# A graph attention layer on one core: index work and node projections become one stage, each partition holds 13 consecutive tiles, and the borders between tiles cross partitions by matrix products

## The reference

```
q, k, v = layer_norm(x @ Wq), layer_norm(x @ Wk), layer_norm(x @ Wv)      # nodes, by head
ke, ve  = layer_norm(edge_attr @ Wke), layer_norm(edge_attr @ Wve)        # edges, by head
rel_k = layer_norm(concat(ke, k[src]) @ relk_W + relk_b)
qk    = sum(q[dst] * rel_k) / 4
lse   = logsumexp of qk over the edges of one dst
rel_v = layer_norm(concat(ve, v[src]) @ relv_W + relv_b)
agg   = segment_sum((qk - lse[dst]) * rel_v, dst)
z     = layer_norm(relu(agg @ z_W + z_b))
out   = layernorm(x + z)
```

## Time and profile before

| | |
|---|---|
| median of 3 runs | 3415.34 us |
| the profiled execution's own time | 3418.76 us |
| its span | 3417.0 us |
| PE busy | 2971.2 us (87% of the span) |
| DVE busy | 3060.6 us (90%) |
| ACT busy | 2326.8 us (68%) |
| POOL busy | 2483.4 us (73%) |
| PE's granted clock, mean | 0.928 of 2.4 GHz |

### The profile page before, as it was taken

How to read it: one execution, slowest core, us unless ns; L and a number is a source line. 1 busy time by engine, 2 the same in 40 slices (tenths; PEclk the granted TensorE clock), 3 DMA queues, 4 the chain that set the end, 5 groups by cost and what they waited for, 6 DMA issues and landing times. The chain is left out here.

```text
span 3417.0 us, 75946 instructions
## 1 busy us (share of the span) xinstructions
PE 2971.2 (87%) x18966; PEld 2581.6 (76%) x19162; DVE 3060.6 (90%) x4202; ACT 2326.8 (68%) x5281; POOL 2483.4 (73%) x1886
## 2 busy tenths in 40 slices
PE   0335599999999999999999999999999999967698
PEld 0313488888888888888888888888888888854465
DVE  5545499999999999999999999999999999987555
ACT  0015478787887888787878788888878887853333
POOL 1527688888888888888888888888888888842660
PEclk6569799999999999999999999999999999998855
DMA  6143588888888888888888888888888888855431
GB/s 81 32 48 119 150 250 248 251 246 250 247 250 247 251 245 251 248 249 249 247 249 248 249 247 251 245 250 247 250 247 250 246 250 248 248 185 159 115 86 42
DMA packets 692637, 723.74 MB, mean 212 GB/s; under 512 B 125638, under 2 KB 586875, under 8 KB 691929
## 3 DMA queue, kind: packets, MB, share of 16 engines
q1 hardware_dynamic: 596163, 503.11, 47.5%
q0 software_dynamic: 84896, 211.67, 23.5%
q10 hardware_dynamic: 11511, 8.18, 1.3%
HBM read 483.77 MB, written 238.10 MB: 211 GB/s over the span
## 5 line engine op out<-in xcount | busy, mean ns | idle before, releaser
L1194 POOL DMA_INDIRECT e_rows<-node_table,e_gcol x1564 | 2178.7, 1393 | 482.2 <-issue 477.4
L1017 PE MATMUL banks<-w_edge,e_eat 128*128 128x240 f32 x6256 | 1399.3, 367 | 3.3 <-DVE e_p L1262 3.0
L1017 PEld LDWEIGHTS banks<-w_edge,e_eat 128*128 128x128 f32 x6256 | 1181.5, 190 | 113.5 <-DVE e_p L1262 11.8
L1010 PE MATMUL banks<-e_h,e_oh 128*128 128x256 f32 x3128 | 826.4, 387 | 8.2 <-ACT e_agg L1095 4.2
L1245 DVE TENSOR_REDUCE e_zs<-e_z 128x96 f32<-128x1440 f32 x391 | 646.2, 1653 | 0.6 <-issue 0.3
L1010 PEld LDWEIGHTS banks<-e_h,e_oh 128*128 128x128 f32 x3128 | 534.1, 191 | 51.9 <-DVE e_h L1270 5.1
L1095 ACT ACTIVATE e_agg<-banks 128x512 f32<-128x512 f32 x782 | 464.9, 594 | 104.3 <-PE banks L1010 104.0
L1280 DVE TENSOR_REDUCE e_yvar<-e_ysq 128x64 f32<-128x960 f32 x391 | 448.1, 1146 | 40.4 <-ACT e_ysq L1125 40.4
L1262 DVE TENSOR_TENSOR e_p<-banks,e_yr 128x960 f32<-128x960 f32 x391 | 448.9, 1148 | 3.2 <-PE banks L1017 3.2
L1270 DVE TENSOR_TENSOR e_h<-e_p,e_zw 128x960 f32<-128x960 f32 x391 | 449.2, 1149 | 0.1
L1210 DVE TENSOR_TENSOR e_p<-e_p,e_rows 128x960 f32<-128x960 f32 x391 | 449.1, 1149 | 0.0
(11 more groups left out here) (369 smaller groups left out, 2794.6 us busy)
## 6 DMA issues: line engine op xcount, KB each, us to landing
tile_sums<-e_agg SPq DMA_DIRECT2D x391, 512.0 KB
e_q<-q_by_rank SPq DMA_DIRECT2D x1564, 96.0 KB
e_ea<-in_edge_attr SPq DMA_DIRECT2D x390, 256.0 KB
e_rows<-node_table,e_gcol POOLq DMA_INDIRECT x1564
edge_lse<-t_lse_sb SPq DMA_DIRECT2D x14, 448.0 KB, 3.4
edge_qk<-e_qkt SPq DMA_DIRECT2D x130, 48.0 KB
node_table<-n_tb SPq DMA_DIRECT2D x24, 240.0 KB
t_x<-edge_qk SPq DMA_DIRECT2D x2, 2240.0 KB
```

The source lines that it names most:

```text
L1010: last = nc.tensor.matmul(agg_ps[:, (j % 2) * AW:(j % 2 + 1) * AW], oh[:, x % OR, j, :], hh[:, x % HR, j, :, :, :].rearrange("p h s d -> p ...
L1017: last = nc.tensor.matmul(out_ps[:, j // 2, (j % 2) * 2 * HC:(j % 2 + 1) * 2 * HC], eat[:, x % 4, j * P:(j + 1) * P], t["w_edge"][:, at:at ...
L1194: g.indirect_dma_start(out=rows[:, k, j, :], out_offset=None, in_=table, in_offset=bass.IndirectOffsetOnAxis(ap=gcol[:, kb, at:at + 1].bit ...
```

## The change

`prologue` and `nodes` become one phase, `start`, with one barrier fewer.

- Layout: partition p holds the 13 consecutive tiles 13p to 13p + 12. Loads are one contiguous run in each partition. A tile's neighbour is mostly the next column of the same partition; at a partition's border the value comes by a PE product with a shifted identity (`identx`). The running sums over tiles are made in each partition (13 long), then over the 128 partition totals in one row, and go back by a product with a one. `tile_ends`, `tile_bases` and `first_edge` in DRAM are gone; the next node's first edge (`lbn_ps`) is a product too.
- The search for a node's tile has 14 columns in place of 129, in three pieces (`PICKS`) in place of 17.
- The gathers of `hits` have a buffer for all 49 blocks in place of three rings of four, and DVE's counting is spread over the turns of the node loop (`SET_AT`). `rank_row` is made in turn 18 (`LB_AT`), and all scatters of q come after it. q's three parts for all nodes are held in `room_b`.
- The node loop is unrolled. The table's bias is added by DVE instead of POOL; the third part of q is written by DVE instead of ACT. Casts of the rank features, the flags, the carry keys and their stores lie in the loop's turns. The weights' evictions and the casts of `dst` and `src` are ACT's.
- `edges`: `e_feat` and `rank_code` have 5 partitions instead of 128; DVE sets them and the other constants, and the load of `e_gcol` goes ahead of the wait for that.

```diff
-            for i in range(3):
-                sp.dma_start(t["tile_d"][i:i + 1, 0:2], below[i:i + 1, :]).then_inc(s_tep, 16)
...
-            for i, (which, at) in enumerate(((0, 2), (0, 1), (0, 3), (1, 2), (1, 1), (1, 0), (2, 2), (2, 1))):
-                sp.dma_start(tl[:, i, :], t["tile_d"][which, at:at + ROWS].rearrange("(k e) -> k e", e=P)).then_inc(s_tl, 16)
...
-            sp.dma_start(t["lb_d"].rearrange("(b p) -> p b", p=P), lb[:]).then_inc(s_lbst, 16)
-            sp.wait_ge(s_lbst, 16)
-            sp.dma_start(lb_next[:, 0:BLOCKS - 1], t["lb_d"][1:1 + whole].rearrange("(b p) -> p b", p=P)).then_inc(s_lbn, 16)
...
+            parts = lambda ap, lo, hi: ap[lo * ROWS:hi * ROWS].rearrange("(p e) -> p e", e=ROWS)
+            sp.dma_start(flat(dst_i[0:LOW]), parts(a["dst"], 0, LOW)).then_inc(s_dst, 16)
...
+            nc.tensor.matmul(shift_ps[:, 0:KT], identx[:, 0:P], lastx[:, 2:KT + 2], start=True, stop=True)
...
+            nc.tensor.matmul(car_ps[:, 0:1], car_row[0:1, 0, 0:P], t["one_c"][0:1, 0:1], start=True, stop=True)
...
+    PICKS = [(0, 12), (12, 36), (36, BLOCKS)]
+    SET_AT = {5 * k // 4 + 2: k for k in range(SETS)}
+    LB_AT = 5 * (SETS - 1) // 4 + 3
...
+                if c == LB_AT:
+                    pe.wait_ge(s_lb, 1)
+                    nc.tensor.matmul(lbn_ps, identx[:, 2:P + 2], lb[:, 0:BLOCKS], start=True, stop=False)
+                    nc.tensor.matmul(lbn_ps, corner[:], lb[0:1, 1:BLOCKS + 1], start=False, stop=True).then_inc(s_lbn, 1)
...
+            pool.wait_ge(s_idx, 1)
+            for n in range(NP):
+                b, nb, rows = pair(n)
+                pool.wait_ge(s_1, n + 1)
+                pool.wait_ge(s_2, n + 1)
+                pool.wait_ge(s_3, n + 1)
+                for b2 in range(b, b + nb):
+                    g.indirect_dma_start(out=t["q_rank"], ..., in_=qp[0:rows, b2, :], ...).then_inc(s_sc, 16)
...
-        nfeat = sb_mid("rank_code", [P, P], bf16)
+        nfeat = sb_mid("rank_code", [5, P], bf16)
...
-    feat = sb("e_feat", [P, FB, BE], bf16)
+    feat = sb("e_feat", [5, FB, BE], bf16)
...
+                        sp.dma_start(gcol[:, kb, :], t["cols"][:, bass.ds(BATCH * TILES * b, BATCH * TILES)]).then_inc(s_ft[kb], 16)
+                        if not loop and c == 0:
                             sp.wait_ge(s_init, INIT)
                         sp.dma_start(feat[0:3, kb, :], t["feat_d"][:, bass.ds(BE * b, BE)]).then_inc(s_ft[kb], 16)
-                        sp.dma_start(gcol[:, kb, :], t["cols"][:, bass.ds(BATCH * TILES * b, BATCH * TILES)]).then_inc(s_ft[kb], 16)
...
-            g.memset(feat[:], 0.0).then_inc(s_init, 1)
-            pool.wait_ge(s_init, 1)
-            g.memset(feat[0:5, :, :], 1.0).then_inc(s_init, 1)
-            g.memset(p[:, :, :, :, :, C:D], 1.0).then_inc(s_init, 1)
-            g.memset(hh[:, :, :, :, 0, C:D], 1.0).then_inc(s_init, 1)
...
+            v.memset(feat[:], 1.0).then_inc(s_init, 1)
+            v.memset(p[:, :, :, :, :, C:D], 1.0).then_inc(s_init, 1)
+            v.memset(hh[:, :, :, :, 0, C:D], 1.0).then_inc(s_init, 1)
```

More of the change, by code:

```diff
@@ new lines, in start @@
+    s_u, s_tb, s_qs, s_q = sem("nodes_scaled"), sem("nodes_table"), sem("nodes_q_scaled"), sem("nodes_q")
+    s_1, s_r1, s_2, s_3 = sem("nodes_part1"), sem("nodes_rest1"), sem("nodes_part2"), sem("nodes_part3")
+    CONSTS, MASKS = 25 + C, 9
+    SMALLS = 5 + 2 + 2 + 10 + 3
+    first = [banks[:, 3 * k:3 * k + 2, :] for k in range(2)]
+    second = [banks[:, 3 * k + 2, :] for k in range(2)]
+    x_ps = banks[:, 6, :]
+    shift_ps, car_ps, e16_ps = bank[2][:, 0:KT + 3], bank[2][:, 3 * P:3 * P + 2], bank[2][:, 3 * P + 8:3 * P + 10]
@@ new lines, in start, with picked, pair @@
+    locT_ps = bank[2][0:1, P:3 * P]
+    rel_ps, col_ps = bank[0][:, 0:4 * C + 4 + D], bank[0][:, P:P + 10]
+    src_ps = [bank[5], bank[6], bank[7], bank[1][:, P:2 * P]]
+    lbn_ps, pre_ps = bank[7][:, 0:BLOCKS], bank[7][:, P:P + 2 * BLOCKS]
+    def picked(b0, b1):
+        w = KT + 1
+        return bank[3 + PICKS.index((b0, b1)) % 2][:, 0:(b1 - b0) * w].rearrange("p (b c) -> p b c", c=w)
+    def pair(n):
+        if not 0 <= n < NP:
+            return None
+        return (2 * n, 2, P) if n < PAIRS else (BLOCKS - 1, 1, LAST)
@@ L294, in _ @@
+            for k in range(3):
+                sp.wait_ge(s_tst[k], 16 * len(range(k, NP, 3)))
+            sp.wait_ge(s_ri, 16)
+            sp.wait_ge(s_ki, 16)
             sp.wait_ge(s_nf, 16 * 5)
-            sp.wait_ge(s_rt, 16 * 2)
+            sp.wait_ge(s_st, 16 * 9)
         @block.gpsimd
@@ L481, in _, with count @@
[L481 to L486 removed]
+            def count(k):
                 nb = min(SLOTS, BLOCKS - SLOTS * k)
                 bs = slice(SLOTS * k, SLOTS * k + nb)
[L489 removed]
+                dve.wait_ge(s_hit[k], 16 * nb)
@@ L714, in body @@
+                last = nc.tensor.matmul(bank[7][:, (2 + i) * HC:(3 + i) * HC], w_ct[:, 3 + i, :], bdg[:, 2 * i, :], start=True, stop=True)
+            last.then_inc(s_prod, 1)
+            pe.wait_ge(s_t, len(PICKS))
+            pe.wait_ge(s_wev, 10)
+            for c in range(NP + 1):
+                n = c - 1
+                if pair(n):
+                    b, nb, rows = pair(n)
                     pe.wait_ge(s_xc, n + 1)
-                    if loop or x >= 2:
+                    if n >= 2:
@@ L718, in body @@
                     for c2 in range(nb):
-                        nc.tensor.matmul(first[k][0:rows, c2, 0:3 * HC + F], xt[:, k, c2, 0:rows], t["w_node"][:, 0:3 * HC + F], start=True, stop=True)
-                        last = nc.tensor.matmul(second[k][0:rows, c2 * 2 * HC:(c2 + 1) * 2 * HC], xt[:, k, c2, 0:rows], t["w_node"][:, 3 * HC + F:NW],
+                        nc.tensor.matmul(first[n % 2][0:rows, c2, 0:3 * HC + F], xt[:, n % 2, c2, 0:rows], t["w_node"][:, 0:3 * HC + F], start=True, stop=True)
@@ L721, in body @@
+                        last = nc.tensor.matmul(second[n % 2][0:rows, c2 * 2 * HC:(c2 + 1) * 2 * HC], xt[:, n % 2, c2, 0:rows], t["w_node"][:, 3 * HC + F:NW],
                                                 start=True, stop=True)
                     last.then_inc(s_pr, 1)
-                if pair(c, i, loop):
-                    n, k, b, nb, rows = pair(c, i, loop)
-                    pe.wait_ge(s_x[k], 16 * use(c, i))
-                    if loop or c >= 1:
+                n = c
+                if pair(n):
+                    b, nb, rows = pair(n)
+                    pe.wait_ge(s_x[n % XR], 16 * (n // XR + 1))
+                    if n >= 1:
```

1040 lines of the change are left out of this document (524 added, 516 removed).

## The result

The changed kernel takes 3450.55 us, the median of 4 runs (3446.07 to 3456.58), against 3416.09 us of the kernel before (4 runs, 3415.11 to 3417.57): 1.0102 times as long, with an interval of 1.0084 to 1.0119. It is slower, as predicted, but by 34 us and not by 88. What follows is read from one profiled execution of each, with spans of 3454.9 and 3417.0 us. The profiled execution of the changed kernel was the slowest of its four, 6 us above the median.

What follows compares the result with a forecast made beforehand. DVE by its work and PE by work and a round trip were taken to bind together. From 3418.8 us, 120 and 7.5 less and 215 more gave 3506, so 3503 us against the median; range 3423 to 3609.

Steps and rivals of the forecast that it cites:

- What bounds: Edges' phase: DVE (99% busy) and PE (96%) bind together; PE's 0.18 us wait a turn is a round trip, no reserve.
- Start, steps 1 to 3: Start phase: comparison at 24 us, search and weight products to the node loop at 67, DVE to turn 18, rank_row at 170.
- the forecast's overlapping rows: Node loop to rank_row: 98 us if neighbouring DVE instructions overlap by some 0.08 us each, 109 otherwise; 103 taken.
- Start, steps 4 and 5: End of start phase: 49 scatters wait for rank_row, last at 233 us; 9.9 us more, edges start at 243, 120 less.
- Start of the edges: Edges' constants: memsets of 128 partitions go, one DVE memset comes; 7.5 us less, bounds 3.5 and 8.5.
- my bracket: Start of the edges: DVE's memset of 6144 bfloat16 columns lies between 2 us and POOL's 5.2.
- The five partitions: PE in the edges' turns: four changes of rows cost 0.55 us a turn, 215 us in all, bounds 156 and 297.
- my lower bound: Four changes of rows in an edge turn: 0.40 us, from shorter bfloat16 loads and 0.04 hidden by the round trip.
- The sum: Whole kernel: 120 and 7.5 us less, 215 more, 3506 us against the profiled execution, 3503 expected.
- Free changes: Rival on PE in the edges' phase: changes of rows cost nothing, 3288 us; chance 0.14.
- 0.10 us each with a reserve of 0.18: Rival on PE in the edges' turns: small changes less reserve add 86 us, 3374 us; chance 0.08.
- The start giving its gain back: Rival in the start phase: counting waits for gathers on DVE, up to 60 us lost, 3563 us; chance 0.06.

Runs made afterwards that it cites:

- e2: Changed kernel with e_feat and rank_code on 128 partitions again, but the products L1108 reading only 5 rows: 3366.81 us, 0.9829 of the kernel before.
- e3: Changed kernel with operands padded to 128 partitions, both places (L1083 and L1108) reading 32 rows: 3448.35 us, 1.0079 of the kernel before.
- e4: Kernel before with only rank_code and e_feat cut to five partitions, old start kept: 3584.54 us, 1.0472 of the kernel before.
- e5: Changed kernel with operands padded to 128 partitions, both places (L1083 and L1108) reading 64 rows: 3451.20 us, 1.0109 of the kernel before.
- e15: Changed kernel, five rows, with products L1108 and L1115 interleaved, ten changes of rows a turn instead of four: 3688.19 us, 1.0794 of the kernel before.
- e7: Changed kernel with 128 partitions again, counting moved earlier and rank_row made in turn 13 instead of 18: 3271.62 us, 0.9577 of the kernel before.
- e14: Changed kernel with 128 partitions again, L1083 alone reading 5 rows, on a chip where the kernel before took 3701.95 us: 3632.07 us, 0.9794.
- e17: Same kernel as e14 on another chip, 128 partitions with L1083 alone reading 5 rows: 3365.52 us, 0.9858 of the kernel before.
- e1: Changed kernel with e_feat and rank_code on 128 partitions again, all else as changed: 3288.89 us, 0.9605 of the kernel before.
- e13: Changed kernel with L1108 and L1115 interleaved, all operands on 128 partitions, on a chip where the kernel before took 3701.95 us: 3657.46 us, 0.9878.
- e12: Changed kernel, five rows, with L1108 and L1115 interleaved, on a chip where the kernel before took 3701.95 us: 3828.51 us, 1.0325.
- e16: Same kernel as e13 on another chip, L1108 and L1115 interleaved with all operands on 128 partitions: 3290.50 us, 0.9633 of the kernel before.

## Why the prediction was right in sign and too high

- *What bounds.* Right. DVE and PE were tied, and PE's round trip was no reserve: in e2 two changes worth 0.20 us by the rows added 0.195 to the turn. In the changed kernel DVE is 965 us busy in 1000 and PE alone sets the turn.
- *Start, steps 1 to 3.* Node loop at 64 us (forecast 67), gathers from 43.8 (44), `rank_row` at 160 (170). The search took 15.97 / 74 = 0.22 us a pass, not 0.26, the price of a pass of 129 columns where these have 14; the weight products began at 52.5 instead of 56.5. They then took 9.4 us and not 6.9: their loads, like those of the search, took 333 ns, as in the kernel before at a granted clock of 0.50 (the view of windows gives 1.00 for this stretch, which these lengths contradict), while the 6.9 had been read from a stretch with a mean clock of 0.71. From the loop's start to `rank_row` it was 96 us, not 103, near the 98 of the forecast's overlapping rows.
- *Start, steps 4 and 5.* The scatter series after `rank_row` is the new wait, as said; it ended at 226. To the first row of the edges it was 14 us, not 9.9. The edges began at 239.1 against 243: -123.5 for a forecast of -120. That it came so close is partly luck: 10 us too many up to `rank_row` stand against 1.4 too few in the scatters and 4.5 too few behind them, and the traces with this start spread over 9 us.
- *Start of the edges.* Forecast -7.5, measured -4.6 by the first gather (10.0 us after the phase's start instead of 14.6) and -2.2 by the first reduction. DVE's memset of five partitions took 5.18 us, POOL's end of my bracket and not DVE's 2.
- *The five partitions.* This step failed in size. I took 0.55 us a turn, because "the rows nearest to it are the two changes at full clock", with some allowance for the shorter loads. The runs showed 0.404, the 0.40 of my lower bound: 0.09 and 0.11 at L1108, 0.09 and 0.16 at L1083, less 0.04 to 0.05 in the round trip. The lower bound had been built rightly (the fp32 price less the difference of the two loads' lengths), and only one of four loads behind a change is fp32. The price went with the length of the load; I took a value some two fifths of the way up to the fp32 one for all four places, where a full-length fp32 load stands at none and the shorter one of the transposes at one. 391 x (0.55 - 0.40) = 58 us too many, +157 where I wrote +215.
- *The sum.* -123.5 - 2.2 + 157.3 + 6.2 + 0.1 = +37.9 for a forecast of +87.5. The 6.2 us at the end of the edges' phase I had not foreseen. They are not due to the change: e3, e4, e5 and e15 have 18.2 us there as before, e7 22.8 with 128 rows, and one and the same kernel had 24.5 us as e14 and 18.3 as e17. They belong to the single execution or its chip; what causes them stays open. Without them the spans differ by 31.7 us, and the medians by 34.5.
- *Rivals.* Free changes: false, though their time is to a microsecond what e1 gives once the changes are gone (3288 and 3289 us); so close is luck, since the start gained more than forecast and the start of the edges less. 0.10 us each with a reserve of 0.18: the price was right, and of the reserve only 0.04 to 0.05 us was there. The start giving its gain back: false; DVE's queue did not wait for gathers (the gathers end at 111 us, and the last set is counted at 153, where its place in the queue is).

## What to carry to other kernels

Before cutting the zero rows off an operand, look whether its product stands between products of full height: the rows saved nothing here, and each change of height between bfloat16 products cost 0.10 us, about the weight load that it laid bare. Zero rows up to 65 took the cost away. Ask for it in the rows of the weight loads (a load that starts with its own product, "issue" ahead of it), multiply by the turns, and price it by the load that follows the change, not by the nearest example of another type. And where a phase ends in a series behind one last value, look at the place of that value in the queue and not only at the work: moving it five turns ahead gave 19 us.

## What the hardware showed that I had not expected

- 64 rows cost a change and 65 do not (7.204 against 6.796 us a turn), while 5, 32 and 64 are alike. An operand of just over half the height is as cheap as a full one, and one of half the height is dear between full ones.
- The partitions did not count in a memset: 6144 bfloat16 columns took 5.18 us on DVE over 5 partitions and over 128 (e1), and four pieces of 1536 columns over 128 partitions 1.34 us each. POOL took 5.22 us over 128 and 5.21 over 5.
- One chip ran the kernel before 8% slower. In the interleaved control with 128 rows there (e13), groups of DVE and PE have the lengths they have elsewhere, while the same waits last longer: e_qkt 19.5 us in 19 waits, the longest 1.8, where e1 has 16.8 in 25 and 0.7. SP's register instructions, 60 to 72 ns each in e1, took up to 722 ns there. What slows that chip stays open.

```profile
L1295 DVE TENSOR_REDUCE e_zs<-e_z 128x96 f32<-128x1440 f32 x135 | 223.1, 1653 | 0.0
L1069 PE MATMUL banks<-w_edge,e_eat 128*128 128x240 f32 x2159 | 485.3, 369 | 0.0
```

```profile
PE banks L1091 <- ACT e_qkt L1222: 19.5, 19, 1.8
```

On that chip part of PE's cost fell into its idle time: the ten changes of e12 looked like 0.50 us over the control, with PE's idle time down from 0.58 to 0.20 us a turn, and were 1.02 us on another chip (e15 against e16).
